# A state-space scan whose input product is contracted over 40 rows, with two banks for its sums

## The chip, the cores and the metric

One core of a Trainium2 chip runs the whole program. It has five engines: TensorE (PE in the profile, PEld for its weight loads), VectorE (DVE), ScalarE (ACT), GpSimd (POOL) and SyncE (SP), which here only issues DMAs. Each engine works through its own instructions in order and waits on semaphores for the others. The metric is the device time of one execution in microseconds. Matmuls read SBUF and write PSUM, which has eight banks of 128 x 512 float32.

## What is computed

Two sequences (B = 2) of L = 2048 steps with 256 channels go through a feed-forward block, a selective state-space block and a second feed-forward block. The middle block is the costly one. Cut to its core:

```python
dt = soft_clamp(softplus(xc @ W_dt.T + b_dt), 0.001, 0.1, 0.5)        # (2, 2048, 512)
Bp, Cp = xc @ W_B.T, xc @ W_C.T                                       # (2, 2048, 16)
dA = exp(soft_clamp(dt[..., None] * A, -8.0, 8.0, 0.5))               # (2, 2048, 512, 16)
def step(h, inp):                                                     # h: (2, 512, 16)
    h = h * dA_t + dB_t * x_t[:, :, None]                             # dB * x = (dt * x) * B
    nrm = sqrt(sum(h * h, axis=(1, 2), keepdims=True))
    fac = minimum(20.0 / (nrm + 1e-08), 1.0)
    h = where(t % 10 == 0, h * fac, h)
    y = einsum('bdn,bn->bd', h, C_t) + D_param * x_t
    return (h, y)
x_out = ys * (gate * sigmoid(gate)) @ W_out.T
```

The state is renormalised every tenth step, so the scan is cut into blocks of ten steps, and no block can start before the norm of the one before it is known.

## The kernel before

The kernel has three stages that hand over to each other. The **first stage** (`pre_stage`) takes 256 steps of both sequences at a time (8 tiles, `TILES`): feed-forward block, projections, convolution, dt, u = dt * x, and B and C in one product of 32 rows (`project_bc`), all stored to scratch DRAM. Its PSUM ring of four banks is filled in the order of the list `order`. The **scan stage** (`scan_stage`) does the recurrence. The **last stage** (`post_stage`) gates, projects, and runs the second feed-forward block.

The scan works in 410 **units** (`UNITS`): unit m is block j = m // 2 of ten steps of sequence b = m % 2. The state of a unit is 128 partitions x 64 rows x 11 places, one of the 11 being the carry from the block before. What each engine does in its turn m, in this order:

- PE: `total(m + 2)`, the sum of squares over partitions; `inputs(m + 2)`, the product u * B of the unit, four matmuls of 176 columns each out of the tile `ub`; if a piece is due, `turn_piece`; then one eighth of a `readout`.
- ACT: `squares(m + 2)`, usually two of the 64 tanh rows of the next chunk (`tanhs`), `decays(m + 4)`, and the copies out of PSUM (`copy_y`, `high_piece`) if due.
- DVE: `carry(m)` (L1135), the first half of the scan (L1145), `clamp(m + 1)` (L1129), the second half; then `low_piece` if due.
- POOL: `norm(m + 1)` (L938), then `weigh(m, 0)` and `weigh(m, 1)` (L948), which multiply the two halves of the new state by C into `hc`; then `mask_piece` if due.

A **readout** sums `hc` over the 16 state columns for a group of four blocks, eight units (`QB * B`), with 16 matmuls against the identity into the PSUM bank `psY`, two of them per unit. It runs one group behind. Its first matmul waits until ACT has copied the sum of the group before it out of the same bank (`y_copied`), and ACT does this copy at the end of the same turn, m % 8 == 0. `hc` has two buffers, so the first `weigh` of a group waits until the readout of two groups before is complete (`y_summed`).

The tile `ub` holds, for each of the ten steps, four rows (`SPLITS`): u and B are each split into a high and a low part, and all four products are summed by the contraction. So 40 of 128 partitions carry data; the other 88 were set to zero once. A row is 512 values of u and 176 of B, B standing at the place of its own step of eleven and zero elsewhere. These rows lie in DRAM (`scratch_ub`) and are made from **pieces** of 128 steps of one sequence: SP loads a piece of u and of B (`load_piece`), PE turns it (`turn_piece`, L835 for u and L836 for B), ACT copies the rounded high part (`high_piece`, L843, 528 columns), DVE subtracts it for the low part (`low_piece`, L847), POOL spreads B by a mask (`mask_piece`, L855), and SP stores all (`store_piece`). There are 32 pieces. Two are made in the first stage, thirty in the scan, one each twelve units (`piece_unit`): in turn m PE and ACT do their part, in turn m + 1 DVE and POOL.

At its block j = 4 SP also stores dt and u of the last tile, 1 MB each (`store_dt_u`). In the last ten units DVE and PE begin work of the last stage (`post.skip`, `post.gate`, `post.project`).

## Time and profile before

| | us |
|---|---|
| median of 3 runs | 1650.04 (1645.67, 1650.04, 1650.18) |
| profiled execution, its own time | 1644.98 |
| its span in the trace | 1643.1 |
| first stage, until the first scan instruction | 430 |
| scan, 410 units | 430 to 1428 |
| rest of the last stage | 1428 to 1643 |

| engine | busy, share of the span | busy in 900 to 1100 us |
|---|---|---|
| PE | 1461.6 (89%) | 173.4 of 200 |
| DVE | 1278.2 (78%) | 170.6 of 200 |
| ACT | 1112.3 (68%) | 165.8 of 200 |
| POOL | 986.4 (60%) | 176.6 of 200 |

The halves of the DVE scan (L1145) take 882 ns each on average, a half of the weighing on POOL (L948) 821 ns, the power for the norm (L938) 551 ns. Granted TensorE clock in the scan is mostly 0.97 to 1.00 of full speed. In the middle of the scan four engines are busy for 83 to 88% of the time, so shares alone don't say which one sets the pace; the order of events does.

### The profile page before, as it was taken

To read this page: it belongs to the slowest core of one execution; us is meant where nothing else is said; L and a number is where in the kernel's file an instruction comes from. 1 tells how busy PE (TensorE), PEld (TensorE's weight loads), DVE (VectorE), ACT (ScalarE), POOL (GpSimd) and SP (SyncE) were. 2 spreads that over 40 slices of the span, in tenths; PEclk is the share of its full clock that TensorE was granted. 3 is DMA by queue.
4 is the path that set the end of the run, shared out by engine and by line. 5 is a ranking of instruction groups with operands and counts; after the bars stand their busy time and mean duration, and the time that the engine had idled before them with its cause. 6 is when DMAs were issued, how large, how long until landed. Compare 5 with 4: busy or idle time off the path is not lost. (4 is left out here: it accounts for less than half of the span.)

```text
span 1643.1 us, 24197 instructions
## 1 busy us (share of the span) xinstructions
PE 1461.6 (89%) x6460; PEld 986.7 (60%) x6460; DVE 1278.2 (78%) x2555; ACT 1112.3 (68%) x2515; POOL 986.4 (60%) x1350
## 2 busy tenths in 40 slices
PE   6999999999688888888888888888888888999998
PEld 5555555554456566656665656665665665677776
DVE  7657656655578888888887888887888889877885
ACT  4355445557978888888887888887888874243333
POOL 1202222012479898989988889898998999700000
PEclk9999999999789999999999999999999999999999
DMA  7222355125565555656655565555655436465430
GB/s 251 77 79 91 117 146 143 66 92 189 164 182 158 162 152 140 172 149 168 160 154 151 137 174 133 158 161 141 178 153 155 135 98 198 122 208 171 137 116 26
DMA packets 232654, 236.84 MB, mean 144 GB/s; under 512 B 46120, under 2 KB 198376, under 8 KB 232520
## 3 DMA queue, kind: packets, MB, share of 16 engines
q1 hardware_dynamic: 231576, 233.99, 49.7%
q8 instruction: 54, 0.88, 0.2%
q10 hardware_dynamic: 944, 1.31, 0.2%
q14 instruction: 80, 0.66, 0.1%
HBM read 136.84 MB, written 98.68 MB: 143 GB/s over the span
## 5 line engine op out<-in xcount | busy, mean ns | idle before, releaser
L1145 DVE TENSOR_TENSOR_SCAN h<-decay,banks 128x352 f32<-128x352 f32 x820 | 710.5, 882 | 56.8 <-POOL hc L948 1.5
L948 POOL TENSOR_TENSOR hc<-h,bc 128x320 f32<-128x320 f32 x820 | 655.1, 821 | 30.6 <-PE banks L995 28.4
L995 PE MATMUL banks<-hc,w_ident 128*128 128x320 f32 (+1 forms) x1664 | 543.6, 452 | 47.6 <-ACT yc L1084 38.6
L1050 ACT ACTIVATE tb<-dtc,a 128x320 f32<-128x320 f32 (+1 forms) x832 | 416.3, 554 | 4.8 <-DVE x L562 4.8
L995 PEld LDWEIGHTS banks<-hc,w_ident 128*128 128x128 f32 x1664 | 291.8, 196 | 125.5 <-POOL hc L948 39.8
L1072 ACT ACTIVATE decay<-tb 128x640 f32<-128x640 f32 x410 | 296.3, 723 | 0.4
L938 POOL TENSOR_TENSOR rc<-qs,w_mhalf 128x1 f32<-128x1 f32 x410 | 225.9, 551 | 114.9 <-DVE qs L1129 106.0
L983 PE MATMUL banks<-ub 128*128 128x176 f32 x1640 | 283.9, 297 | 10.9 <-DMA ub<-scratch_ub 10.9
L976 PEld LDWEIGHTS banks<-sc_ss,sc_ones 128*128 128x128 f32 x820 | 134.6, 197 | 263.8 <-ACT sc_sq L1061 246.2
L1061 ACT ACTIVATE sc_sq<-h 128x64 f32<-128x64 f32 x410 | 128.1, 313 | 189.1 <-issue 100.0
L983 PEld LDWEIGHTS banks<-ub 128*128 128x128 f32 x1640 | 227.4, 201 | 12.2 <-DMA ub<-scratch_ub 11.2
L976 PE MATMUL banks<-sc_ss,sc_ones 128*128 128x1 f32 x820 | 151.4, 254 | 90.4 <-ACT sc_sq L1061 56.4
L244 POOL TENSOR_TENSOR ln_rz<-ln_vz,w_mhalf 128x4 f32<-128x4 f32 x8 | 13.9, 1736 | 281.0 <-DVE ln_vz L568 281.0
L1135 DVE TENSOR_SCALAR banks<-h,rc 128x64 f32<-128x64 f32 x410 | 136.6, 333 | 34.2 <-POOL rc L938 22.2
L330 PE MATMUL banks<-zT,win 128*128 128x512 f32 x256 | 115.3, 604 | 5.5 <-ACT gf L397 4.5
L338 PE MATMUL banks<-xc,wdt 128*128 128x512 f32 x256 | 112.4, 592 | 3.1 <-ACT sg L434 3.1
L1284 POOL TENSOR_TENSOR q_ln_rs<-q_ln_ve,w_mhalf 128x4 f32<-128x4 f32 x8 | 10.9, 1364 | 172.2 <-DVE q_ln_ve L1555 172.2
L1385 ACT ACTIVATE q_gf<-banks,w_b,w_a 128x512 f32<-128x512 f32 x64 | 49.9, 780 | 69.6 <-PE banks L1318 67.9
L330 PEld LDWEIGHTS banks<-zT,win 128*128 128x128 f32 x256 | 48.1, 192 | 68.2 <-issue 60.3
L338 PEld LDWEIGHTS banks<-xc,wdt 128*128 128x128 f32 x256 | 48.0, 190 | 58.6 <-issue 54.1
L1129 DVE TENSOR_SCALAR qs<-banks 128x1 f32<-128x1 f32 x410 | 55.5, 135 | 30.3 <-PE banks L976 30.0
L1061 ACT ACTIVATION_READ_ACCUMULATOR sc_sq<-h 128x1 f32 x410 | 77.0, 188 | 0.0
(117 smaller groups left out, 1562.1 us busy)
## 6 DMA issues: line engine op xcount, KB each, us to landing
ub<-scratch_ub SPq DMA_DIRECT2D x410, 107.5 KB
bc<-scratch_blk SPq DMA_DIRECT2D x205, 160.0 KB, 3.6
scratch_ub<-turned SPq DMA_DIRECT2D x64, 512.0 KB, 4.1
scratch_ub<-spread SPq DMA_DIRECT2D x64, 176.0 KB, 4.3
scratch_xc<-xc SPq DMA_DIRECT2D x8, 1024.0 KB, 4.8
scratch_sg<-sg SPq DMA_DIRECT2D x8, 1024.0 KB, 5.9
scratch_dt<-dt SPq DMA_DIRECT2D x8, 1024.0 KB, 5.9
scratch_u<-u SPq DMA_DIRECT2D x8, 1024.0 KB, 6.7
```

Of the source, the lines that this page charges most:

```text
L330: mm = pe.matmul(out, win[:, k, (m0 + m) * P:(m0 + m + 1) * P], zT[:, k, :], start=(k == 0), stop=(k == KD - 1))
L338: mm = pe.matmul(out, wdt[:, k, m * P:(m + 1) * P], xc[:, i % 2, k, :], start=(k == 0), stop=(k == KE - 1))
L938: pool.tensor_tensor(rc[:, b:b + 1], qs[:, b:b + 1], w.mhalf[:, 0:1], ALU.pow).then_inc(norm_ready, 1)
L948: pool.tensor_tensor(hc[:, pl % 2, x * kh * B * N:(x + 1) * kh * B * N, j % QB * S:(j % QB + 1) * S] .rearrange("p (c b n) e -> p c b n e" ...
L976: pe.matmul(psQ[:, b:b + 1], ones[:], ss[:, b:b + 1], start=True, stop=True).then_inc(sum_ready, 1)
L983: mm = pe.matmul(psI[m % B][:, c * N * W:(c + 1) * N * W], ub[m % URING][:, c * P:(c + 1) * P], ub[m % URING][:, E:], start=True, stop=True)
L995: mm = pe.matmul(psY[:, 0:KE * B * wide], w.ident[:], rhs, start=(n == 0), stop=(n == N - 1))
L1050: act.activation(tanh_rows(c, r), dtc[:, c % 2, k * B:(k + 1) * B, 0:blocks_of(c) * S].rearrange("p b (k e) -> p k b e", e=S), ACT.Tanh, s ...
L1061: act.activation(sq[:, b, :], state(m - B)[:, :, S], ACT.Square, accum_out=ss[:, b:b + 1]).then_inc(sq_ready, 1)
L1072: act.activation(decay[:, m % DRING].rearrange("p (g i e) -> p g i e", g=DB, e=W)[:, :, :, 1:], tanh_block(j, b), ACT.Exp, scale=DTA_HALF ...
L1135: dve.tensor_scalar(inp(m)[:, :, 0], state(m - B)[:, :, S], rc[:, b:b + 1], None, ALU.mult).then_inc(carry_ready, 1)
L1145: dve.tensor_tensor_scan(state(m).rearrange("p r e -> p (r e)")[:, half], decay[:, m % DRING, half], psI[m % B][:, half], 0.0, ALU.mult, A ...
```

## The change

- **40 rows.** `ub` has 40 partitions instead of 128, so `inputs` contracts over 40. The four memsets of 128 x 688 go.
- **Two sum banks.** `readout` p writes bank 2 or bank 5 in turns (`y_bank`) and waits for the copy of p - 2 (`y_before`). Bank 2 comes from the pieces, which now have bank 3 alone. `copy_y` moves from turns m % 8 == 0 to m % 8 == 2. At the end of the scan, after `LAST_EVEN`, only bank 5 is used.
- **Late weighing.** POOL weighs unit m - 1 in turn m, in one instruction of four by 16 by 10 instead of two of half the size. The parts of a readout move one turn later with it.
- **B from the first stage.** A new ring entry `("bt", i, 0)` in which PE turns B of a tile (four transposes of 16 rows, `turn_b`), ACT copies it (`copy_bt`), and POOL splits and spreads it (`spread_b`: a copy, a subtraction, four masks for each tile), around `norm2`. SP stores it (`store_b`). For the last tile the four masks are in POOL's turns 8, 12, 16 and 20 of the scan. A piece is now u alone, 512 columns, with no mask.
- **Pieces.** One each ten units. In its turn m and the three after it PE does one transpose each, after the readout; ACT copies 256 columns each in turns m + 4 and m + 5; DVE subtracts in turn m + 6.
- **SP.** dt and u of the last tile go out in eight stores of 256 KB at j = 1 to 8 (`store_last`).

```diff
@@ the first stage
+        if i >= 1:
+            order.append(("bt", i - 1, 0))
...
+            if i >= 2:
+                scan.store_b(sp, i - 2, 2, G)
+            if i >= 1:
+                scan.store_b(sp, i - 1, 0, 2)
             sp.wait_ge(xc_ready, 2 * (i + 1))
...
+            if i >= 1:
+                scan.spread_b(pool, i - 1, 0, 2)
             if i + 1 < TILES:
                 norm2(i + 1)
-            if i in (6, 7):
-                scan.mask_piece(pool, i - 6)
+            if i >= 1:
+                scan.spread_b(pool, i - 1, 2, G)
...
+        def turn_b(i):
+            out = fill(("bt", i, 0))
+            pe.wait_ge(ring_read, use["bc", i, 0] + 1)
+            for q in range(G):
+                mm = pe.transpose(out[:, q * N:(q + 1) * N], bcs[0:N, q * P:(q + 1) * P], w.ident[0:N, 0:N])
+            mm.then_inc(ring_done, 1)
@@ the scan
-    return 12 * (k - B) + 2
+    return 10 * (k - B)
...
+    return 2 if p % B == 0 and p <= LAST_EVEN else 5
...
+    return p - 2 if p <= LAST_EVEN + 1 else p - 1
...
-    ub = [own.put(f"ub{q}", [P, ROW], F32R) for q in range(URING)]
+    ub = [own.put(f"ub{q}", [SPLITS * S, ROW], F32R) for q in range(URING)]
...
+        for q in range(q0, q1):
+            if G * i + q >= 2:
+                pool.wait_ge(b_out[q % 2], 2 * 16 * ((G * i + q) // 2))
+            pool.tensor_tensor(
+                spread[:, q % 2], bts[:, :, q].bitcast(F32).unsqueeze(3).broadcast_to([P, 2, N, W]),
+                mask[:, (i * TT // P + q % 2) % (S // 2)].unsqueeze(1).unsqueeze(1).broadcast_to([P, 2, N, W]),
+                ALU.mult).then_inc(spread_done, 1)
...
-            if j == 4:
-                pre.store_dt_u(sp, TILES - 1)
+            if 1 <= j <= 2 * KE:
+                pre.store_last(sp, j - 1)
+            if j in (6, 8, 10, 12):
+                store_b(sp, TILES - 1, j // 2 - 3, j // 2 - 2)
...
-            weigh(m, 0)
-            weigh(m, 1)
-            if m - 1 in pieces:
-                mask_piece(pool, pieces[m - 1])
+            if m >= 1:
+                weigh(m - 1)
+            if m in (8, 12, 16, 20):
+                spread_b(pool, TILES - 1, m // 4 - 2, m // 4 - 1)
...
-                if p >= 1:
-                    pe.wait_ge(y_copied, p)
+                if y_before(p) >= 0:
+                    pe.wait_ge(y_copied, y_before(p) + 1)
...
-            p, part = m // (QB * B) - 1, m % (QB * B)
+            p, part = (m - 1) // (QB * B) - 1, (m - 1) % (QB * B)
             if p >= 0:
                 readout(p, part * each, (part + 1) * each)
...
+            for c in range(KE):
+                if m - c in pieces:
+                    turn_piece(pe, pieces[m - c], psT, c, c + 1)
...
-            if m % (QB * B) == 0 and m >= 2 * QB * B:
+            if m % (QB * B) == 2 and m >= 2 * QB * B:
                 copy_y(m // (QB * B) - 2)
-            if m in pieces:
-                high_piece(act, pieces[m], psT)
+            for x in range(2):
+                if m - KE - x in pieces:
+                    high_piece(act, pieces[m - KE - x], psT, x * E // 2, (x + 1) * E // 2)
...
-            if m - 1 in pieces:
-                low_piece(dve, pieces[m - 1], psT)
+            if m - KE - 2 in pieces:
+                low_piece(dve, pieces[m - KE - 2], psT)
```

On PE, in the scan, a piece stood in one turn. Before (L976 is `total`, L983 `inputs`, L835 and L836 the piece, L995 the readout):

```order
L976 MATMUL banks<-sc_ss,sc_ones 128x1
L983 MATMUL banks<-ub_100 128x176 x4
L835 MATMUL banks<-w_ident,piece 128x128 x4
L836 MATMUL banks<-w_ident,piece_b 128x32
L995 MATMUL banks<-hc,w_ident 128x320 x2
L976 MATMUL banks<-sc_ss,sc_ones 128x1
L983 MATMUL banks<-ub_101 128x176 x4
```

And now (L1060 is `total`, L1067 `inputs`, L1079 the readout, L897 one transpose of the piece):

```order
L1067 MATMUL banks<-ub_100 128x176 x4
L1079 MATMUL banks<-hc,w_ident 128x320 x2
L897 MATMUL banks<-w_ident,piece 128x128
L1060 MATMUL banks<-sc_ss,sc_ones 128x1
L1067 MATMUL banks<-ub_101 128x176 x4
L1079 MATMUL banks<-hc,w_ident 128x320 x2
L897 MATMUL banks<-w_ident,piece 128x128
L1060 MATMUL banks<-sc_ss,sc_ones 128x1
L1067 MATMUL banks<-ub_102 128x176 x4
```

The transposes stand one to a turn, behind the readout and not ahead of it; the order of total, inputs and readout is the same.

On POOL, in the scan, before (L938 is `norm`, L948 a half of `weigh`, L855 the mask of a piece):

```order
L938 TENSOR_TENSOR rc<-qs,w_mhalf 128x1
L948 TENSOR_TENSOR hc<-h,bc_97 128x2x16x10 x2
L938 TENSOR_TENSOR rc<-qs,w_mhalf 128x1
L948 TENSOR_TENSOR hc<-h,bc_97 128x2x16x10 x2
L855 TENSOR_TENSOR spread<-turned,mask 128x352
L938 TENSOR_TENSOR rc<-qs,w_mhalf 128x1
```

And now (L1021 is `norm`, L1032 `weigh`):

```order
L1032 TENSOR_TENSOR hc<-h,bc_99 128x4x16x10
L1021 TENSOR_TENSOR rc<-qs,w_mhalf 128x1
L1032 TENSOR_TENSOR hc<-h,bc_96 128x4x16x10
L1021 TENSOR_TENSOR rc<-qs,w_mhalf 128x1
L1032 TENSOR_TENSOR hc<-h,bc_96 128x4x16x10
```

One instruction stands between two norms where two stood, and the mask of the piece is gone from the row.

On ACT, in the scan, before (L843 is the copy of a piece, L1061 `squares`, L1050 the tanh rows, L1072 `decays`):

```order
L1072 ACTIVATE decay<-tb 128x64x10
L843 ACTIVATE turned<-banks 128x528
L1061 ACTIVATE sc_sq,sc_ss<-h 128x64
L1050 ACTIVATE tb<-dtc,a_110 128x16x2x10 x2
L1072 ACTIVATE decay<-tb 128x64x10
```

And now (L906, L1147, L1136, L1158 in the same sense):

```order
L1158 ACTIVATE decay<-tb 128x64x10
L906 ACTIVATE turned<-banks 128x256
L1147 ACTIVATE sc_sq,sc_ss<-h 128x64
L1136 ACTIVATE tb<-dtc,a_111 128x32x10 x2
L1158 ACTIVATE decay<-tb 128x64x10
L906 ACTIVATE turned<-banks 128x256
```

The copy of a piece is in two halves, a turn apart.

## Rows read from the trace of the kernel before

**Rows 1.** Timeline, one undisturbed unit: start, us, engine, line, what [idle before <-releaser].
```profile
955.99 0.34 DVE L1135 TENSOR_SCALAR banks<-h,rc 128x64 f32<-128x64 f32 x1
956.14 0.32 ACT L1061 ACTIVATE sc_sq<-h 128x64 f32<-128x64 f32 x1 [0.17 <-issue]
...
956.60 0.30 PEld L976 LDWEIGHTS banks<-sc_ss,sc_ones 128*128 128x128 f32 x2 [0.63 <-ACT sc_sq L1061]
...
957.26 0.13 DVE L1129 TENSOR_SCALAR qs<-banks 128x1 f32<-128x1 f32 x1
...
957.35 1.27 PE L995 MATMUL banks<-hc,w_ident 128*128 128x320 f32 x4
...
957.54 0.55 POOL L938 TENSOR_TENSOR rc<-qs,w_mhalf 128x1 f32<-128x1 f32 x1
...
958.12 0.34 DVE L1135 TENSOR_SCALAR banks<-h,rc 128x64 f32<-128x64 f32 x1
...
958.73 0.30 PEld L976 LDWEIGHTS banks<-sc_ss,sc_ones 128*128 128x128 f32 x2 [0.62 <-ACT sc_sq L1061]
```

**Rows 2.** Timeline, the start of a group of eight units.
```profile
982.56 0.33 DVE L1135 TENSOR_SCALAR banks<-h,rc 128x64 f32<-128x64 f32 x1
...
983.23 1.58 POOL L948 TENSOR_TENSOR hc<-h,bc 128x320 f32<-128x320 f32 x2 [0.70 <-PE banks L995]
...
985.13 1.31 PE L995 MATMUL banks<-hc,w_ident 128*128 128x320 f32 x4 [1.06 <-ACT yc L1084]
...
985.36 0.34 DVE L1135 TENSOR_SCALAR banks<-h,rc 128x64 f32<-128x64 f32 x1 [0.60 <-POOL rc L938]
```

**Rows 3.** Timeline, a unit in which a piece of u is turned.
```profile
997.37 0.60 PE L835 MATMUL banks<-w_ident,piece 128*128 128x128 f32 x4
...
997.90 0.13 PEld L836 LDWEIGHTS banks<-w_ident,piece_b 32*128 32x128 f32 x1 [0.17 <-issue]
...
998.08 1.34 PE L995 MATMUL banks<-hc,w_ident 128*128 128x320 f32 x4
...
998.18 0.61 ACT L843 ACTIVATE turned<-banks 128x528 fp32r<-128x528 f32 x1
...
998.83 0.71 DVE L847 TENSOR_TENSOR turned<-banks,turned 128x528 fp32r<-128x528 f32 x1 [0.61 <-ACT turned L843]
```

**Rows 4.** Timeline, a group of eight that begins just after a piece.
```profile
1003.71 0.34 DVE L1135 TENSOR_SCALAR banks<-h,rc 128x64 f32<-128x64 f32 x1
...
1004.15 2.28 PE L995 MATMUL banks<-hc,w_ident 128*128 128x320 f32 x4 [1.05 <-ACT yc L1084]
...
1007.75 0.34 DVE L1135 TENSOR_SCALAR banks<-h,rc 128x64 f32<-128x64 f32 x1
```

**Rows 5.** Busy us of PE, PEld, DVE, ACT, POOL (xcount), PEclk, DMA share, GB/s.
```profile
594.00:596.00 2.00, 1.69 (x4) 1.19 (x5) 1.09 (x2) 2.00 (x6) 1.39 (x2) 0.69 0.61 129
...
1294.00:1296.00 2.00, 2.00 (x8) 1.45 (x7) 0.86 (x3) 1.50 (x3) 0.88 (x2) 0.62 0.10 36
```

**Rows 6.** Instructions of L1135, 442 to 1427 us: ns min/median/max, first and last start.
```profile
L1135 DVE TENSOR_SCALAR banks<-h,rc x406: 322/333/342, 442.1 to 1426.4; 128x64 f32<-128x64 f32 x136
```

**Rows 7.** Who waited for whom, 442 to 1427 us: us in total, times, longest.
```profile
PE banks L995 <- ACT yc L1084: 38.0, 36, 1.1
...
DVE turned L847 <- ACT turned L843: 21.9, 30, 1.8
```

**Rows 8.** Groups by line and shape: busy us, mean ns | idle before.
```profile
L855 POOL TENSOR_TENSOR spread<-turned,mask 128x352 fp32r<-128x352 f32 x32 | 25.9, 809 | 8.2 <-DVE turned L847 8.2
...
L1084 ACT ACTIVATE yc<-banks 128x320 f32<-128x320 f32 x51 | 21.2, 416 | 15.3 <-PE banks L995 15.3
...
L253 POOL TENSOR_TENSOR ln_s<-ln_mv,ln_rs 128x4 f32<-128x4 f32 x8 | 1.7, 212 | 0.0
```

**Rows 9.** Timeline, early in the scan: PE waits for the rows of a unit.
```profile
464.40 0.69 PE L983 MATMUL banks<-ub 128*128 128x176 f32 x4 [4.39 <-DMA ub<-scratch_ub]
```

**Rows 10.** Timeline, first stage: PE before the gate projection.
```profile
253.56 7.13 PE L330 MATMUL banks<-zT,win 128*128 128x512 f32 x16 [0.60 <-ACT gf L397]
```

More of the change, by code:

```diff
@@ L142, in store_dt_u, with store_last, stored @@
         store(sp, "u", u[:], u_out, i)
+    def store_last(sp, k):
+        name, tile, ready, done = ("dt", dt, dt_ready, dt_out) if k < KE else ("u", u, u_ready, u_out)
+        c = k % KE
+        sp.wait_ge(ready, LAST + 1)
+        sp.dma_start(dram[name][:, c * B:(c + 1) * B, steps(LAST)],
+                     tile[:, c, :].rearrange("p (b t) -> p b t", b=B)).then_inc(done, 16)
+    def stored(i):
+        return 16 * (i + 1) if i < LAST else 16 * (LAST + KE)
     def dt_u(dve, i):
@@ L218, in sync @@
                 scan.load_units(sp)
+                scan.store_b(sp, LAST - 1, 2, G)
             if i == 3:
@@ L364, in tensor @@
             project(i, "x", 0)
+            if i >= 1:
+                turn_b(i - 1)
             if 1 <= i < LAST:
@@ L377, in tensor @@
             if i in (5, 6):
-                scan.turn_piece(pe, i - 5, psD.rearrange("p k c -> p (k c)"))
+                scan.turn_piece(pe, i - 5, psD[:, 0], 0, KE)
         project_bc(LAST)
+        turn_b(LAST)
     def scalar(act, scan, post):
@@ L485, in scalar @@
                 copy_x(i, 0, KE)
+                if i >= 1:
+                    copy_bt(i - 1)
             else:
@@ L493, in scalar @@
                 copy_x(i, 3, KE)
+                copy_bt(i - 1)
                 scan.tanhs(act, 0, 20, 33)
@@ L523, in scalar @@
         copy_bc(LAST)
-        scan.tanhs(act, 0, 52, KE * N)
+        scan.tanhs(act, 0, 52, 54)
+        copy_bt(LAST)
+        scan.tanhs(act, 0, 54, KE * N)
     def vector(dve, scan, post):
@@ L646, in vector @@
                 apply2(i + 1)
+            if i == 0:
+                scan.masks(dve)
             if i == 4:
                 scan.decay_scale(dve)
-                scan.masks(dve)
                 post.residual_steps(dve)
-    return Pre(sync, gpsimd, tensor, scalar, vector, dt_u, store_dt_u, order, use,
+    return Pre(sync, gpsimd, tensor, scalar, vector, dt_u, store_last, stored, order, use,
                ring_done, ring_read, sg_out, xc_out, r_out, u_out, dt_out, bc_out, u_ready, r_ready, x1_ready, t2_done,
@@ L673 @@
 ROW = E + N * W
+LAST_EVEN = (UNITS - 6) // (QB * B) - 2
+assert LAST_EVEN % 2 == 0
 Scan = namedtuple("Scan", """sync gpsimd tensor scalar vector load_first load_units tanhs decay_rates decay_scale masks
-    decay_ready y_out y_copied squares load_piece turn_piece high_piece low_piece mask_piece store_piece ut_lo""")
+    decay_ready y_out y_copied squares load_piece turn_piece high_piece low_piece store_piece ut_lo
+    spread_b store_b copy_bt b_split""")
 def chunk_of(j):
@@ L827, in load_piece @@
         sp.dma_start(piece[:], dram["u"].rearrange("p (c b) t -> p c b t", b=B)[:, :, b, t:t + P]).then_inc(piece_in, 16)
-        sp.dma_start(piece_b[:], dram["bc"][:, b, t:t + P]).then_inc(piece_in, 16)
-    def turn_piece(pe, k, out):
-        pe.wait_ge(piece_in, 32 * (k + 1))
-        if k >= 1:
-            pe.wait_ge(ut_lo, k)
-        for c in range(KE):
-            pe.transpose(out[:, c * P:(c + 1) * P], piece[:, c, :], w.ident[:])
-        pe.transpose(out[:, E:E + 2 * N], piece_b[:], w.ident[0:2 * N, 0:2 * N]).then_inc(ut_done, 1)
@@ L861, in store_piece @@
         t, b = k // B * P, k % B
[L862 removed]
         sp.wait_ge(ut_lo, k + 1)
         for r in range(2):
[L865 to L869 removed]
+            sp.dma_start(dram["ub"][b, t:t + P, 2 * r:2 * r + 2, 0:E], turned[:].bitcast(F32)).then_inc(ut_out, 16)
@@ L871, in masks, with store_b @@
+    def store_b(sp, i, q0, q1):
+        for q in range(q0, q1):
+            t = i * TT + q % 2 * P
+            sp.wait_ge(spread_done, G * i + q + 1)
+            for half in range(2):
+                sp.dma_start(
+                    dram["ub"][q // 2, t:t + P].rearrange("t (r h) x -> t r h x", h=2)[:, :, half, E:],
+                    spread[:, q % 2].bitcast(F32).rearrange("p r n e -> p r (n e)")).then_inc(b_out[q % 2], 16)
     def masks(dve):
-        for q in range(URING):
-            dve.memset(ub[q][:].bitcast(F32), 0.0).then_inc(ub_zero, 1)
@@ L908, in sync @@
                     load_unit(sp, m)
[L909 to L912 removed]
+            if j - 3 in after and after[j - 3] + 1 < PIECES:
+                load_piece(sp, after[j - 3] + 1)
             if j + RING - 1 < NB:
```

159 lines of the change are left out of this document (88 added, 71 removed).

## The prediction

> **What bounds the kernel now.** The scan fills about 1000 of 1643 us and holds nearly all of the change, so I read it first, in order of time, and not by busy shares, which are alike for four engines. [rows 1] is one undisturbed unit. DVE's carry begins at 955.99 and the next at 958.12, a period of 2.13 us, and DVE has no idle time in it. The others nearly fill the same period. ACT idles 0.17. PE's readout starts at 957.35, takes 1.27 and so ends at 958.62, and its next sum of squares starts at 958.73: a gap of 0.11, and since consecutive matmuls overlap by 0.07 (the four transposes of [rows 3] end at 997.97, the next matmul starts at 997.90), PE has about 0.18 to spare. The clamp starts 0.66 after the sum of squares, which takes about 0.4 of it, so a late sum costs DVE nothing up to about 0.25. POOL's norm starts at 957.54, 0.28 after the clamp, and ends at 958.09, just before the carry: POOL has next to nothing to spare.
>
> So DVE sets a floor of 2.13 us a unit. The 406 carries of [rows 6] span 984.3 us, or 2.43 for each of 405 periods. At 2.13 they would take 862.7. The remaining 121.6 us is what the change can touch. Read by the gaps between carries, it comes in few sizes:
>
> - Pieces, thirty. DVE waits 0.61 for ACT's copy, then works 0.71 [rows 3]; 1.30 on the carries. The wait was there 30 times [rows 7]. 30 x 1.30 = 39.
> - Starts of a group of eight, 51 of them by the count of L1084 [rows 8]. POOL's first weighing waits 0.70 for the readout to leave `hc`, so the norm and then the carry come late: from 982.56 to 985.36 is 2.80, 0.67 over the floor [rows 2]. 51 x 0.67 = 34.
> - In the same place PE waits 1.06 for ACT's copy of the old sum [rows 2], 36 times in the scan [rows 7]. In [rows 2] this costs nothing beyond the 0.67: DVE is late by POOL's delay anyway. It costs where a piece has just gone by [rows 4]: PE has idled before, the wait comes on top, and the four readout matmuls take 2.28 instead of 1.27. The carries are 4.04 apart, 1.91 over the floor, with some 0.1 behind it. The granted clock shows why: 0.69 and 0.62 of full speed, parts of the stretch at the lower level of 1.2 GHz [rows 5]; these two are the first and the last of 12 such places. Each costs about 1.3 more than an ordinary start: 12 x 1.3 = 16.
> - The last ten units, in which DVE already works for the last stage: 10. A start-up with late DMAs: 6; PE waited 4.39 for its rows [rows 9]. The rest, about 16, is late loads and units with four tanh rows.
>
> **The change part by part**, against the profiled execution's own 1645.0 us (span 1643.1 and 1.9 around it).
>
> *Late weighing in one instruction.* The two halves take 1.58 [rows 2]. A product of four columns on POOL takes 0.212 [rows 8], so most of 0.2 per instruction is fixed; taking 0.19, one instruction of both halves takes 1.45, 0.13 less. In an undisturbed unit this is worth nothing, as DVE is the floor. At a group's start it is worth 0.13, if POOL's wait stays. It stays: weighing and readout both move a turn later, so the weighing of unit 8n still stands one turn behind the readout that must clear `hc`.
>
> *40 rows.* The data and columns are the same, so I take no time off. What could be added is the passage between products of 40 and of 128 rows, twice a unit. The nearest row is the turning of B, 32 rows, among products of 128 [rows 3]: its weights are loaded after a gap of 0.17; its matmul starts at 997.90, 0.20 after the fourth transpose (997.37 and three steps of 0.11), and the readout's 0.18 after that, where transposes follow each other at 0.11. Both passages cost 0.20 + 0.18 - 0.22 = 0.16. Bounds are nothing and twice the 0.17 gap, 0.34. I take 0.16, measured on the same kind of passage. It fits into PE's 0.18, so the floor stays at 2.13, but the readout ends 0.16 later. At a group's start this gives -0.13 + 0.16 = +0.03, over 51 starts **+1.5**.
>
> Against this: the Trainium skill, "TensorE: Matmul & The Clock Gate", section "LDWEIGHTS (loading the stationary operand)", gives the load's time by columns and not by the rows contracted. The trace agrees for the load itself (0.13 with 32 rows), not for the gap ahead of it. By the rule alone the sum would have nothing for the passage; that is the first rival below.
>
> *Pieces.* DVE's wait of 0.61 goes: it subtracts a turn after the second copy. Its own 0.71 remains (0.69 for 512 of 528 columns). ACT's halves: 0.416 for 320 columns [rows 8] and 0.61 for 528 [rows 3] give 0.36 for 256. Less ACT's 0.17 a turn, ACT is late by 0.19, then 0.38, of which 0.25 is covered: 0.13 on DVE. PE's four transposes, 0.11 each on a queue with 0.02 left, come to 0.36 late, 0.11 beyond that cover, partly at once with ACT's. I take 0.9 a piece: 30 x (0.9 - 1.3) = **-12**. Ends: -18 (only the wait goes) and 0.
>
> *Two sum banks.* PE's wait of 1.06 goes in all 51 starts, but only the 12 places with the low clock are on the path. There PE would idle 0.7 for the piece and 0.7 for POOL, not twice about 1.05. I take ten of the twelve as gone: **-13**. Ends: -16 and 0.
>
> *Masks and B.* The 30 masks leave POOL in the scan, where they hid behind DVE's wait. The last tile's four return, 0.81 each [rows 8], with two small ones ahead. POOL has 0.04 + 0.13 to spare a unit: 4 x 0.64 + 0.5 = **+3**. In the first stage PE gets a `turn_b` per tile: four transposes of 16 rows, 0.20 + 3 x 0.11 + 0.18 = 0.7. In six tiles PE waits 0.60 before the gate projection for a gelu [rows 10], whose time DVE sets; that wait shrinks by as much. 6 x 0.1 + 2 x 0.7 = **+2**. On POOL two masks, 1.6, come ahead of the next `rstd1`; DVE then gets its rows just before it would wait for ACT's copy of x anyway. SP's waits in `store_b` stand ahead of `store_xc`, which is ready long after. If these covers fail, 1.6 a tile, 10 in all.
>
> *SP.* dt and u of the last tile in eight stores instead of 2 MB at once: the late rows of [rows 9] should mostly be in time. **-4** (0 to -6).
>
> *Ends.* `copy_bt` adds 0.3 to ACT ahead of the first unit. The readout lags one turn more: 1.2 when the scan ends. In the last six units, which PE bounds, 6 x 0.16 = 1. **+2.5**.
>
> Sum: 1.5 - 12 - 13 + 3 + 2 - 4 + 2.5 = -20, so 1625. The profiled execution lies at the low end of the runs shown (1645.7 to 1650.2), and the time to come may lie at either; half the difference, 2, gives **1627**.
>
> **The rivals.**
>
> *Free passages.* If 40 rows cost nothing, each start gains 0.13 (-6.6 instead of +1.5), a piece costs 0.83 (-14), and the two ends save 2: 1615. For it: the rule cited above. Against it: the gap in [rows 3]. With all covers holding and all twelve places gone, 1604.
>
> *The slow places stay.* The 12 places with the low clock remain because piece, group start and the passages still fall together: 1625 + 13 + 2 = 1640. For it: pieces now come every ten units and meet a group's start in many phases.
>
> *PE becomes the bound (slower).* If each passage costs a whole gap of 0.17, PE needs 2.13 - 0.18 + 0.34 = 2.29 a unit. 405 x 0.16 = 65 over the floor, and 120 transposes x 0.11 = 13. DVE then has 0.16 + 0.25 in hand at each of 81 pieces and starts, which gives back 33. Net +45 - 20 = +25: 1672. The kernel is slower than before once the passages cost more than about 0.26 a unit. Against it: the trace's matmuls moved by 0.16 in all, though with 32 columns and not 176 in flight.
>
> *The clock falls for lack of rows.* If a product of 40 rows keeps the array less occupied in the eyes of what grants the clock, every group start can become like [rows 4]: 39 more at 1.3 and none of the twelve gone, 1627 + 13 + 51 = 1691, and far more if it stays low. For it: the drops show that the scan is not far from it. The Trainium skill, same page, Part 1, says the clock follows "how busy the PE has been recently"; by that, rows don't matter and this doesn't happen. No row here shows a long stretch of products of few rows.
>
> *The change does not do what it says.* That PE's wait for the copy is off the path in most groups is already in the sum.
>
> **How the numbers follow.** Forecast (1610 to 1636) 0.44; free passages 0.26; slow places stay 0.11; PE the bound 0.12; clock 0.07. Below 1604 lies under 0.05. To leave out no more than 2 in 10, the range reaches up to most of the case with PE as the bound: 1604 to 1662. A change of 0.3%, about what a measurement of this kernel can tell from none, is 5 us: same is 1645 to 1655. Faster: the first three less a little, 0.76. Same, from the slow places and a half-costly passage, 0.09. Slower 0.15.
>
> **What would show it.** Carries 2.13 apart in undisturbed units: the floor holds; 2.2 or more throughout, with DVE idle for PE: PE is the bound. In `inputs`, a gap before the weight load of the first matmul and of the readout behind it: the passage. At a group's start: no PE wait for ACT, POOL still waiting 0.7 to 0.9 for PE, a carry 0.7 late. At a piece: no DVE wait for ACT, about 0.9. Weighing: one instruction of about 1.45. Few stretches below full clock after 480 us. First stage longer by about 2. I am wrong if DVE gains or loses work, if the granted clock falls often, or if POOL's new work in the first stage delays DVE.

## The result, and the profile after

| | us |
|---|---|
| before, median of 4 runs | 1648.47 (1645.67 to 1650.18) |
| after, median of 4 runs | 2191.14 (2189.95 to 2195.20) |
| ratio after / before, 95% interval | 1.330 (1.327 to 1.333) |
| profiled execution of after, its span | 2190.14, 2188.3 |
| predicted | 1627 (1604 to 1662) |

The kernel became 33% slower. From the page of after: busy time by engine; the granted clock of PE in 40 slices of the span, in tenths; shares of the chain that ended last, by engine; and three groups of instructions.

```profile
PE 2139.6 (98%) x6460; PEld 1520.6 (69%) x6460; DVE 1341.0 (61%) x2551; ACT 1123.6 (51%) x2553; POOL 934.1 (43%) x956
...
PEclk9999999955555555555555555555555555559999
...
PE 77%; DVE 2%; ACT 0%; issue 0%; POOL 0%; DVEq 0%; POOLq 0%; ACTq 0%
...
L1032 POOL TENSOR_TENSOR hc<-h,bc 128x640 f32<-128x640 f32 x410 | 591.1, 1442 | 138.7 <-PE banks L1079 133.6
...
L1067 PE MATMUL banks<-ub 40*128 40x176 f32 x1640 | 470.1, 435 | 0.0
...
L1216 DVE TENSOR_SCALAR qs<-banks 128x1 f32<-128x1 f32 x410 | 64.4, 157 | 463.8 <-PE banks L1060 463.7
```

PE is busy 98% of a span that is 545 us longer. Its instructions are not more, but slower: the four matmuls of a product take 1.16 us (below), where they took 0.69 in [rows 9]. DVE now waits 463.7 us in all for the sum of squares of L1060. The stretches show when (us of PE, PEld, DVE, ACT, POOL, granted clock, DMA share, GB/s):

```profile
0.00:450.00 450.00, 414.94 (x1366) 235.76 (x1366) 280.35 (x578) 252.70 (x388) 125.81 (x134) 0.98 0.47 148
450.00:500.00 50.00, 45.88 (x133) 34.89 (x133) 32.41 (x62) 34.04 (x88) 31.32 (x35) 0.50 0.51 165
...
1000.00:1300.00 300.00, 300.00 (x818) 221.01 (x818) 174.81 (x323) 162.17 (x419) 154.07 (x157) 0.50 0.34 99
...
1960.00:2188.00 228.00, 218.80 (x998) 171.02 (x998) 166.08 (x336) 75.24 (x107) 20.74 (x17) 0.99 0.39 124
```

From 430 us, where the scan begins, to 1963, a few us before its last carry, PE is granted 0.50, its lower level of 1.2 GHz, and in the middle it is busy 300 of 300 us. The first and the last stage run at full clock, as in before. The timeline of one unit of after, to be laid beside [rows 1]:

```profile
1701.12 0.43 PE L1060 MATMUL banks<-sc_ss,sc_ones 128*128 128x1 f32 x2
1701.48 1.16 PE L1067 MATMUL banks<-ub 40*128 40x176 f32 x4
...
1702.57 2.50 PE L1079 MATMUL banks<-hc,w_ident 128*128 128x320 f32 x4
...
1704.86 0.42 PE L1060 MATMUL banks<-sc_ss,sc_ones 128*128 128x1 f32 x2
```

The starts are 0.36, 1.09 and 2.29 apart, 3.74 from one sum of squares to the next, where DVE's floor is 2.13. All carries of after (ns min/median/max, first and last start):

```profile
L1222 DVE TENSOR_SCALAR banks<-h,rc x410: 309/334/339, 433.5 to 1970.2; 128x64 f32<-128x64 f32 x137
```

Between the first and the last of its 410 carries after spends 1536.7 us. In before it is 998.1, from 428.3 to the 1426.4 of [rows 6].

### The profile page after: what moved, and what is told of

The parts are those of the page before. It is cut to its first block, busy times and chain, and to the rows that moved or that the text cites. A ratio compares the mean times of both kernels' runs of the same rounds, so it can differ in the third digit from the quotient of the medians.

```text
span 2188.3 us, 24473 instructions
## 1 busy us (share of the span) xinstructions
PE 2139.6 (98%) x6460; PEld 1520.6 (69%) x6460; DVE 1341.0 (61%) x2551; ACT 1123.6 (51%) x2553; POOL 934.1 (43%) x956
## 4 chain that ended last, share of the span: by engine, by line
PE 77%; DVE 2%; ACT 0%; issue 0%; POOL 0%; DVEq 0%; POOLq 0%; ACTq 0%
PE banks L1079 45%; PE banks L1067 20%; PE banks L1060 4%; PE banks L1384 3%; PE banks L1405 2%; PE banks L1415 2%; PE banks L897 1%; DVE q_ln_st L1637 0%; DVE q_g L1546 0%; DVE q_x L1518 0%; PE banks L1425 0%; PE banks L1394 0%; DVE q_g L1544 0%; DVE q_ln_mv L1640 0%; DVE h L1232 0%
## 5 line engine op out<-in xcount | busy, mean ns | idle before, releaser
L1079 PE MATMUL banks<-hc,w_ident 128*128 128x320 f32 (+1 forms) x1664 | 1006.8, 760 | 0.6 <-ACT yc L1170 0.6
L1232 DVE TENSOR_TENSOR_SCAN h<-decay,banks 128x352 f32<-128x352 f32 x820 | 722.4, 882 | 55.5 <-ACT decay L1158 1.4
L1032 POOL TENSOR_TENSOR hc<-h,bc 128x640 f32<-128x640 f32 x410 | 591.1, 1442 | 138.7 <-PE banks L1079 133.6
L1079 PEld LDWEIGHTS banks<-hc,w_ident 128*128 128x128 f32 x1664 | 477.2, 317 | 222.5 <-issue 219.0
L1021 POOL TENSOR_TENSOR rc<-qs,w_mhalf 128x1 f32<-128x1 f32 x410 | 226.4, 552 | 620.5 <-DVE qs L1216 620.5
L1147 ACT ACTIVATE sc_sq<-h 128x64 f32<-128x64 f32 x410 | 129.1, 315 | 702.5 <-issue 659.8
L1067 PE MATMUL banks<-ub 40*128 40x176 f32 x1640 | 470.1, 435 | 0.0
L1136 ACT ACTIVATE tb<-dtc,a 128x320 f32<-128x320 f32 (+1 forms) x832 | 415.2, 552 | 4.9 <-DVE x L605 4.8
L1067 PEld LDWEIGHTS banks<-ub 40*128 40x128 f32 x1640 | 377.1, 318 | 6.1
L1060 PEld LDWEIGHTS banks<-sc_ss,sc_ones 128*128 128x128 f32 x820 | 259.0, 335 | 159.2 <-issue 145.6
L1216 DVE TENSOR_SCALAR qs<-banks 128x1 f32<-128x1 f32 x410 | 64.4, 157 | 463.8 <-PE banks L1060 463.7
L1158 ACT ACTIVATE decay<-tb 128x640 f32<-128x640 f32 x410 | 295.7, 722 | 0.4
L1060 PE MATMUL banks<-sc_ss,sc_ones 128*128 128x1 f32 x820 | 175.7, 284 | 11.4 <-ACT sc_sq L1147 10.8
L1147 ACT ACTIVATION_READ_ACCUMULATOR sc_sq<-h 128x1 f32 x410 | 76.6, 187 | 0.0
```

Of the source, the lines that this page charges most:

```text
L1021: pool.tensor_tensor(rc[:, b:b + 1], qs[:, b:b + 1], w.mhalf[:, 0:1], ALU.pow).then_inc(norm_ready, 1)
L1032: pool.tensor_tensor(hc[:, pl % 2, :, j % QB * S:(j % QB + 1) * S] .rearrange("p (c b n) e -> p c b n e", c=KE, b=B)[:, :, b], state(m)[:, ...
L1060: pe.matmul(psQ[:, b:b + 1], ones[:], ss[:, b:b + 1], start=True, stop=True).then_inc(sum_ready, 1)
L1067: mm = pe.matmul(psI[m % B][:, c * N * W:(c + 1) * N * W], ub[m % URING][:, c * P:(c + 1) * P], ub[m % URING][:, E:], start=True, stop=True)
L1079: mm = pe.matmul(banks[:, y_bank(p), 0:KE * B * wide], w.ident[:], rhs, start=(n == 0), stop=(n == N - 1))
L1136: act.activation(tanh_rows(c, r), dtc[:, c % 2, k * B:(k + 1) * B, 0:blocks_of(c) * S].rearrange("p b (k e) -> p k b e", e=S), ACT.Tanh, s ...
```

## The experiments

Three theories stood at the start. *Rows*: the clock stays down because the product uses 40 of the array's 128 rows. *Passages*: each change between products of different row counts stalls PE, and it is these short stalls that hold the clock down. *Another part*: the new order, with piece transposes spread over four turns, keeps PE from getting ahead. Below, "after128" is the changed kernel with the product over 128 rows again, and diffs are against it unless said otherwise. A time without a range was measured once.

### Back to 128 rows

Diff against after (left out: the waits on `mask_zero` go up by `URING` to match, and SP waits for it before its first loads):

```diff
-    ub = [own.put(f"ub{q}", [SPLITS * S, ROW], F32R) for q in range(URING)]
+    ub = [own.put(f"ub{q}", [128, ROW], F32R) for q in range(URING)]
...
-        sp.dma_start(ub[m % URING][:].bitcast(F32),
+        sp.dma_start(ub[m % URING][0:SPLITS * S, :].bitcast(F32),
...
+        for q in range(URING):
+            dve.memset(ub[q][:].bitcast(F32), 0.0).then_inc(mask_zero, 1)
```

> The changed kernel with one thing undone: the product u*B is contracted over 128 rows again, 88 of them zeros set once; late weighing, two sum banks, B from the first stage and the spread pieces stay. The result is complete. Theory (the 40 rows hold the granted clock at the lower level, 0.50 in the changed kernel's scan): the clock returns to 0.97 or more and the time is near the 1627 us of the forecast, 1605 to 1640. Rival (something else in the change keeps the clock low, such as the order of the matmuls, the single transposes or the missing waits): the clock stays near 0.5 and the time stays above 2100 us.

Measured: **1604.34** (1603.75 to 1609.19), 0.974 of before (0.971 to 0.978). Everything but the 40 rows gains 2.6%; the 40 rows alone cost 587 us. Granted clock by slice and the group of its weighings:

```profile
PEclk9999999999969999999999999999999999899999
...
L1035 POOL TENSOR_TENSOR hc<-h,bc 128x640 f32<-128x640 f32 x410 | 594.0, 1449 | 32.3 <-PE banks L1082 32.0
```

and all its carries (ns min/median/max, first and last start):

```profile
L1225 DVE TENSOR_SCALAR banks<-h,rc x410: 309/333/346, 435.1 to 1385.0; 128x64 f32<-128x64 f32 x137
```

The first and last carry are now 949.9 apart, 586.8 less than in after: the whole difference lies in the scan.

Where the two part can be seen, since both enter the scan at 0.50: the clock falls at 430 in after and at 435 in after128. After, at the start of the scan, where PE is all but idle:

```profile
434.00:438.00 4.00, 0.58 (x3) 0.57 (x3) 2.69 (x4) 3.97 (x10) 0.18 (x1) 0.50 0.54 134
```

Windows of after128:

```profile
464.00:468.00 4.00, 4.00 (x13) 3.02 (x13) 3.17 (x7) 3.04 (x8) 3.25 (x5) 0.50 0.28 91
468.00:472.00 4.00, 4.00 (x23) 3.14 (x22) 3.42 (x8) 3.67 (x11) 2.93 (x4) 0.89 0.79 236
```

and of after in the same place:

```profile
464.00:468.00 4.00, 4.00 (x12) 2.90 (x11) 2.72 (x5) 3.31 (x9) 2.52 (x3) 0.50 0.48 155
468.00:472.00 4.00, 4.00 (x13) 2.94 (x12) 2.17 (x4) 2.75 (x8) 2.62 (x3) 0.50 0.33 102
```

In both, PE has stopped waiting by 464 and is busy in full. With 128 rows its clock rises in the next window, with 40 it stays down for the rest of the scan. The other kernels below part in the same way: all that use 96 or 128 rows here, and before too, rise for the first time between 458 and 476 us, the one with 64 rows at 521, and those with 40 rows, in all four matmuls of a product or in three, not for hundreds of us.

### Before, with 40 rows alone

Diff against before:

```diff
-                mm = pe.matmul(psI[m % B][:, c * N * W:(c + 1) * N * W], ub[m % URING][:, c * P:(c + 1) * P],
-                               ub[m % URING][:, E:], start=True, stop=True)
+                mm = pe.matmul(psI[m % B][:, c * N * W:(c + 1) * N * W], ub[m % URING][0:SPLITS * S, c * P:(c + 1) * P],
+                               ub[m % URING][0:SPLITS * S, E:], start=True, stop=True)
```

> The kernel before with one thing changed: the product u*B is contracted over the 40 rows that hold data; the tile stays 128 rows with its zeros, and nothing else moves. The result is complete. Theory (40 rows alone do it): the clock falls to 0.5 in the scan and the time is 2150 to 2250 us. Rival (it needs the other parts of the change as well): clock about 0.97 and 1640 to 1670 us.

Measured: **2162.79**, 514 over before, with the mean clock at 0.665. The new order is not the cause.

Its clock is low from 428 to 1937 us, but not without a break. It rises at 1083, 1203 and 1247 and stays up for 34, 3 and 31 us. The first of these:

```profile
1080.00:1084.00 4.00, 4.00 (x15) 2.76 (x14) 1.81 (x4) 2.44 (x6) 2.38 (x4) 0.58 0.10 28
1084.00:1090.00 6.00, 6.00 (x30) 4.15 (x29) 5.60 (x13) 4.57 (x14) 5.58 (x9) 1.00 0.47 123
```

So 40 rows make a rise rare here, not impossible. Each of the three follows within about 4 us the start of a piece's four transposes (1080.17, 1198.87, 1243.63), which have 128 rows; in after, where they stand one to a turn, there is no rise at all. Most of the thirty pieces bring none, and whether the transposes are the cause was not tried.

### 40 rows from the middle of the scan on

Here, and in the reverse of it below, `ub` has 128 partitions as in after128.

```diff
+        def rows(m):
+            return P if m < 200 else SPLITS * S
...
-                mm = pe.matmul(psI[m % B][:, c * N * W:(c + 1) * N * W], ub[m % URING][:, c * P:(c + 1) * P],
-                               ub[m % URING][:, E:], start=True, stop=True)
+                mm = pe.matmul(psI[m % B][:, c * N * W:(c + 1) * N * W], ub[m % URING][0:rows(m), c * P:(c + 1) * P],
+                               ub[m % URING][0:rows(m), E:], start=True, stop=True)
```

> The changed kernel, contracting over 128 rows with zeros up to unit 199 and over 40 rows from unit 200 on. The result is complete. If a steady scan at 40 rows cannot hold the upper level of the clock, it falls within some us of unit 200 and stays low: about 1627 + 210 x 1.3 = 1900 us. If 40 rows only keep a clock that is low from rising again, the fall comes at the first later disturbance (a piece with a group's start, or a late load), some 50 us or more after unit 200. If neither holds, about 1627 us.

Measured: **1861.50**. The first product of 40 rows starts at 898.96. The windows after that:

```profile
920.00:968.00 48.00, 44.59 (x216) 32.09 (x215) 43.04 (x87) 42.41 (x112) 40.51 (x43) 1.00 0.55 160
968.00:972.00 4.00, 4.00 (x14) 2.97 (x14) 3.04 (x7) 3.56 (x9) 2.81 (x3) 0.62 0.88 283
...
1000.00:1600.00 600.00, 600.00 (x1620) 444.30 (x1619) 353.39 (x647) 304.23 (x790) 312.16 (x319) 0.50 0.29 81
```

PE alone, a wait after which the clock stays up, and the one after which it falls:

```profile
938.34 0.38 PE L1063 MATMUL banks<-sc_ss,sc_ones 128*128 128x1 f32 x2 [0.92 <-ACT sc_sq L1153]
...
965.97 0.38 PE L1063 MATMUL banks<-sc_ss,sc_ones 128*128 128x1 f32 x2 [0.84 <-ACT sc_sq L1153]
...
969.04 2.50 PE L1085 MATMUL banks<-hc,w_ident 128*128 128x320 f32 x4
```

A high clock is kept for 70 us with 40 rows, PE busy 44.6 of 48 us, and undisturbed units are 2.13 apart. It falls after PE has waited 0.84, and does not come back in 600 us of unbroken work. The length of that wait alone doesn't explain the fall: a wait of 0.92 had passed without one 28 us before. With 128 rows waits of this size do less: between 480 and 1340 us after128's PE waits 0.8 to 1.6 more than thirty times, and its clock falls once (at 882, after 1.63) and is back in 3.4 us.

### 40 rows first, 128 from the middle on

The same edit the other way round (`SPLITS * S if m < 200 else P`).

> The changed kernel, contracting over 40 rows up to unit 199 and over 128 rows with zeros from unit 200 on: the reverse of the run that changed to 40 rows at unit 200. The result is complete. Theory (40 rows can keep an upper clock but not raise a low one; 128 rows raise it): the clock is low from the start of the scan to about unit 200, then rises within some us and stays up: 1604 + 200 x 1.35 = 1870 to 1900 us. Rival (once low for long it stays low whatever follows): about 2190 us.

Measured: **1888.45**. The first product of 128 rows starts at 1181.87:

```profile
1178.00:1182.00 4.00, 4.00 (x14) 3.04 (x12) 2.17 (x4) 1.95 (x5) 1.95 (x2) 0.50 0.45 157
1182.00:1186.00 4.00, 4.00 (x19) 3.16 (x18) 3.40 (x7) 2.24 (x7) 2.98 (x4) 0.79 0.22 59
1186.00:1190.00 4.00, 3.99 (x23) 2.95 (x22) 3.73 (x7) 3.65 (x11) 3.14 (x4) 1.00 0.46 95
```

PE is as busy before as behind. Only the rows change, and the clock rises within 2 us. With the run before, this shows that it is the rows, whichever units they are in.

### 64 and 96 rows

`ub` has 64 or 96 partitions instead of 128, the rest zeros as in after128.

> The changed kernel with the product contracted over 64 rows, 24 of them zeros. The result is complete. If what counts is the groups of 32 rows that are touched, 40 rows already touch two groups, so 64 rows give the same as 40: clock 0.5, about 2190 us. If it is the number of rows, 64 stands between 40 and 128 and may do better: part of the scan at the upper level, 1640 to 2100 us.

> The changed kernel with the product contracted over 96 rows, 56 of them zeros. The result is complete. With 40, 64 and 128 rows the time was 2191, 2070 and 1604 us. Theory (the number of rows in the array counts, gradually): 96 rows hold the upper level nearly always, 1604 to 1640 us. Rival (anything short of all 128 rows lets the clock fall in large parts of the scan): 1750 us or more.

Measured: **2069.97** with 64 rows (mean clock 0.703) and **1605.59** with 96 (0.978), which is after128's time. Clock by slice, 64 rows first:

```profile
PEclk9999999965656555555555957965555555569999
```

```profile
PEclk9999999999969999999999999999999998899999
```

With 64 rows the clock rises here and there, stays up for 14 to 96 us, and falls again. With 96 it behaves as with 128.

### One matmul of four with 128 rows

Diff against after, with `ub` of 128 partitions as in after128; `inputs` takes `rows(c)` partitions for its matmul c:

```diff
+        def rows(c):
+            return P if c == 0 else SPLITS * S
```

> The changed kernel; of the four matmuls of each product one is contracted over 128 rows (88 zeros), three over 40. The mean is 62 rows. The result is complete. Theory (rows are summed over the work done): as with 64 rows in all four, about 2070 us with some stretches at the upper level. Rival (one product of 128 rows right behind the sum is enough to keep the array counted as full): clock 0.97 and about 1610 us. Other rival (each matmul of few rows is what counts): 2150 us or more, no stretch at the upper level.

Measured: **2248.01**, mean clock 0.646, and no stretch in which the clock rises. The passages of row counts are two a unit, as in after, but the first now stands inside the product: from the sum to the readout PE takes 1.58 where after takes 1.43, and 409 times this 0.15 is 60, about the 57 us that the run is over after. Whether rows are added up over matmuls, with 248 here a little short of the 256 of the 64-row run, or are looked at in another way, these two runs don't tell.

### Passages without few rows

A matmul of 40 rows and 2 columns ahead of each product, overwritten by it:

```diff
+                if c == 0:
+                    pe.matmul(psI[m % B][:, 0:2], ub[m % URING][0:SPLITS * S, 0:P],
+                              ub[m % URING][0:SPLITS * S, E:E + 2], start=True, stop=True)
```

> The changed kernel with 128 rows, and ahead of each product one more matmul of 40 rows and 2 columns, whose result is overwritten by the product. It makes PE pass from 128 rows to 40 and back once a unit, as the contraction over 40 rows does, with all real products at 128 rows. Theory (the rows of the products keep the clock up or not, the passages cost 0.17 us of PE time a unit): clock 0.95 or more, 1604 to 1680 us, passages plus 0.1 for the extra matmul on an engine with 0.18 to spare. Rival (the gaps at the passages are what lets the clock fall): clock near 0.5, above 2100 us.

Measured: **1635.43**, 31 over after128, with the mean clock at 0.969 against 0.981. The clock is nowhere near 0.50 as a whole, so passages alone don't hold it down, and the theory of passages falls. They do not leave it alone either. Here PE is busy in full at 0.50, in a stretch that after128 runs at full clock:

```profile
896.00:920.00 24.00, 24.00 (x72) 18.66 (x72) 12.83 (x25) 11.93 (x31) 10.23 (x11) 0.50 0.26 61
```

In all the clock is low for 55 us after 480, against 20 in after128. So in this one run, with every product at 128 rows, the passages or the small matmul itself seem to make a fall last longer; which of the two wasn't tried. They add 0.28 a unit here (medians of undisturbed units), no less than the real ones do, which makes this a fair test of them. The price of the real ones at full clock, first from after128, PE alone:

```profile
641.09 0.38 PE L1063 MATMUL banks<-sc_ss,sc_ones 128*128 128x1 f32 x2
...
641.34 0.66 PE L1070 MATMUL banks<-ub 128*128 128x176 f32 x4
...
641.84 1.27 PE L1082 MATMUL banks<-hc,w_ident 128*128 128x320 f32 x4
```

and from the kernel with 40 rows from the middle on, while its clock was still at 1.00:

```profile
942.94 0.38 PE L1063 MATMUL banks<-sc_ss,sc_ones 128*128 128x1 f32 x2 [0.34 <-ACT sc_sq L1153]
...
943.25 0.68 PE L1073 MATMUL banks<-ub 40*128 40x176 f32 x4
...
943.87 1.34 PE L1085 MATMUL banks<-hc,w_ident 128*128 128x320 f32 x4
```

The steps are 0.25 and 0.50 with 128 rows, 0.31 and 0.62 (mostly 0.61) with 40, and the four readout matmuls take 1.34 instead of 1.27. Each unit so has three losses, 0.06, 0.11 and 0.07: 0.25 from the sum to the start of the last readout matmul (1.83 instead of 1.58, medians of undisturbed units). With 96 rows all of this is as with 128.

### One sum bank

```diff
-    return 2 if p % B == 0 and p <= LAST_EVEN else 5
+    return 5
...
-    return p - 2 if p <= LAST_EVEN + 1 else p - 1
+    return p - 1
...
-            if m % (QB * B) == 2 and m >= 2 * QB * B:
+            if m % (QB * B) == 1 and m >= 2 * QB * B:
```

> The changed kernel with 128 rows (1604 us), and with one sum bank again: every readout in bank 5, its first matmul waits for the copy of the sum before, which ACT makes at the end of turn m % 8 == 1. The result is complete. The forecast's term for the second bank was 13 us (10 of 12 places with a fallen clock): 1612 to 1622 us, with PE waits of about 1 us for ACT's copy in some 50 places and a clock that falls in about ten. Rival (the wait is off the path since DVE or POOL is late anyway): 1602 to 1608 us.

Measured: **1635.08** (1628.38 to 1638.38), 31 more than after128 in medians, 24 to 34 between the ends of its range and that median. Its waits, 442 to 1427 us (us in all, times, longest):

```profile
PE banks L1082 <- ACT yc L1173: 45.5, 43, 1.1
...
DVE qs L1219 <- PE banks L1063: 27.9, 37, 1.8
```

In after128 the first wait is gone and the second is 9.6 in all, 19 times; in before DVE waited 27.9 for the sum too, 34 times. After 480 us the clock is below full at 13 places with one bank, and at three with two.

### Weighing in two halves

The product into `hc` by two instructions of 320 columns instead of one of 640.

> The changed kernel with 128 rows (1604 us), with the weighing in two instructions of half the size again; it still stands a turn late. The result is complete. The forecast had one instruction 0.13 us shorter than two, worth 0.13 only at group starts: 51 x 0.13 = 7 us more at most, 1606 to 1613 us. Rival (POOL sets the pace, as it has almost nothing to spare): 410 x 0.13 = 50 us more, about 1655 us.

Measured: **1611.04** (1609.93 to 1613.31), 6.7 more in medians; the nearest runs of the two kernels are 0.7 apart and the farthest 9.6. One instruction takes 1.449 (L1035 above), the two took 1.58 [rows 2].

### A piece in one turn

All four transposes of a piece in one turn, and ACT's copy and DVE's subtraction as in before; first with the transposes behind the readout, as this diff of PE's part has it, then ahead of it:

```diff
-            for c in range(KE):
-                if m - c in pieces:
-                    turn_piece(pe, pieces[m - c], psT, c, c + 1)
+            if m in pieces:
+                turn_piece(pe, pieces[m], psT, 0, KE)
```

> The changed kernel with 128 rows (1604 us), with a piece in one turn again: four transposes on PE and one copy of 512 columns on ACT in turn m, the subtraction on DVE in turn m + 1, still every ten units. The result is complete. The forecast had 0.4 us a piece for the spreading: 30 x 0.4 = 12 us more, 1613 to 1622 us, and a DVE wait of about 0.6 us for ACT at each piece. Rival (what a piece gained came with the mask that left POOL): 1602 to 1608 us.

> As the run with a piece in one turn (1654 us, 2.2 us a piece), but with the four transposes ahead of the turn's readout, where the kernel before had them, and not behind it. The result is complete. Theory (the loss there came from the transposes standing behind the readout, 1.2 us, which ACT's copy and then DVE waited for): a piece costs 1.3 us as before the change, DVE waits about 0.6 for ACT, 1613 to 1622 us; the difference to 1604 is what the spreading is worth. Rival (ACT is late for another reason, such as its copy of the sums a turn later): about 1654 us again.

Measured: **1654.31** (8 runs, 1650.30 to 1657.98) behind and **1618.40** (1618.03 to 1620.16) ahead. Who waited, 442 to 1427 us, behind first:

```profile
DVE turned L912 <- ACT turned L907: 55.9, 30, 5.1
...
ACT turned L907 <- PE banks L898: 38.2, 28, 4.6
```

```profile
DVE turned L912 <- ACT turned L907: 25.7, 29, 4.0
```

and of after128, from its first carry to its last:

```profile
DVE turned L912 <- ACT turned L907: 6.6, 28, 0.7
```

Spreading a piece over turns is worth 14 us against one turn with the transposes ahead of the readout, as in before. Behind the readout they cost 36 more: ACT waits for them, and DVE for ACT.

### The readout ahead of its last turn

The eight turns of a readout take 3, 2, 2, 2, 2, 2, 2 and 1 of its matmuls, so that `hc` comes free earlier relative to POOL's first weighing (the last group, behind the loop, starts one matmul later to match):

```diff
-                readout(p, part * each, (part + 1) * each)
+                readout(p, part * each + (part > 0), (part + 1) * each + (part < QB * B - 1))
```

> The changed kernel with 128 rows (1604 us), with the sixteen matmuls of a readout spread over its eight turns as 3, 2, 2, 2, 2, 2, 2, 1 and not two in each. The result is complete. POOL's first weighing of a group waits for the last of them; it ends about 0.6 us sooner. If that wait is what still costs about 0.55 us at each of 51 group starts, 15 to 25 us are gained: 1580 to 1590 us. Rival (PE has no room for a third matmul, 0.6 us, in the first turn and DVE waits there instead): 1600 to 1610 us.

Measured: **1601.28** (1597.71 to 1601.80), 0.970 of before (0.968 to 0.973), the fastest of all. The waits, 442 to 1427 us:

```profile
POOL hc L1035 <- PE banks L1082: 9.8, 37, 2.0
...
DVE qs L1219 <- PE banks L1063: 15.4, 24, 1.5
```

POOL's wait falls from 29.7 in after128 (434 to 1386 us) to 9.8, as expected, but DVE's for PE rises from 9.6 to 15.4: a turn with three readout matmuls fills PE, and the clock is below full more often (44 us in all after 480 us, against 20). So of the 15 to 25 us expected only 3 came; the intervals of the two ratios overlap, though the runs don't (after128's fastest is 1603.75).

## Why the prediction was wrong, step by step

**The step that failed** is "40 rows. The data and columns are the same, so I take no time off", with the passage as the only possible cost. It priced the edit by what PE executes and not by what clock it executes at. The fourth rival had the mechanism, but its price of 1691 let the clock fall at 39 more group starts and come back each time. What happened is its last clause, "far more if it stays low": the clock is low when the scan begins, since it falls at 427 to 436 us in all of these kernels, where PE waits for up to 4 us at a time, and with 40 rows it does not rise. The sum then is not one of stalls. A unit takes PE about 3.74 instead of DVE's 2.13; 409 times 3.74 is 1530, and 1536.7 was measured. This price could have been worked out ahead, by doubling PE's 1.95 in [rows 1] (2.13 less the 0.18 to spare) to 3.9, and the 0.07 it stood at was far too low for a term with no row behind it.

In rows: the clock is 0.50 over 300 us with PE busy 300 of 300. The Trainium skill, "TensorE: Matmul & The Clock Gate", Part 1, says the clock follows "how busy the PE has been recently"; read as busy time, as the prediction read it, this is contradicted. Its section "Why this matters for your kernels" says a lone matmul of 32 rows takes the time of one of 128; that agrees at equal clock (0.68 for four of 40 rows, 0.66 of 128), and not here as a whole (1.16 for four of 40 rows at the lower level).

**The rest of the change** was read nearly right. after128 has no passages, so by the prediction's own terms it is the case of free passages, 1615; 1604 was measured. What the carries take over 2.13 us each, in us:

| | before | after128 |
|---|---|---|
| thirty pieces | 43.0 | 28.6 |
| starts of a group of eight (units m with m % 8 = 1 or 2) | 48.7 | 18.9 |
| first units | 9.2 | 5.8 |
| last 18 units | 10.3 | 14.7 |
| the rest | 15.7 | 10.7 |
| all | 126.9 | 78.7 |

Of these 48 us the first stage takes 7 back: the first carry comes at 428.3 in before and at 435.1 in after128. By the prediction's terms:

- *Passages*: mis-sized, 0.25 a unit and not 0.16. The two gaps are right (0.17), but the 0.07 by which the readout behind them is longer was left out, though [rows 3] has it, 1.34 against the 1.27 of [rows 1]. The Trainium skill's rule that a weight load takes its time by columns (the same page, "LDWEIGHTS (loading the stationary operand)") gives none of the 0.25. PE's slack was taken too small as well: from the start of the last readout matmul to that of the next sum it is 0.55 in after128's undisturbed units, and 0.27 where nothing is waited for, so 0.28 was to spare and not 0.18. The two errors cancel: with 40 rows at full clock a unit kept its 2.13, with 0.03 left. That the floor held is partly luck.
- *Pieces*: 0.88 in the median without passages, 0.83 forecast for that case; 14 us gained, 14 forecast there.
- *Late weighing*: 1.449 against 1.45, and 6.7 us for the two halves against 51 x 0.13 = 6.6. Where a group start costs anything it is mostly 0.53, by the forecast 0.67 - 0.13 = 0.54; but many cost nothing, and all of them together 18.9 us, where 51 x 0.54 is 28.
- *Two sum banks*: mis-sized. 24 to 34 against 13, with 16 as the end. All twelve places with a low clock did go, but one bank costs elsewhere too: DVE waits 27.9 us for the sum of squares, in before as with one bank, and 9.6 with two banks. The prediction had booked PE's wait of [rows 2] at nothing wherever POOL was late as well. The run with one bank has pieces every ten units, not every twelve, so its 31 us need not be what before lost by it.
- *Masks and B*: +2 for the first stage was too little, its end comes 7 late (5 in after). What of that are the transposes, the masks or the copy of B wasn't tried. The last tile's four masks, put at +3, make DVE wait for POOL's norm three times near the start of the scan, 0.98, 0.48 and 0.48: about 2.
- *Ends*: the last 18 units lose 4.4, forecast 2.5 with passages and less without. Why wasn't tried.
- *SP*: the first units gain 3.4, forecast 4.
- *PE as the bound*: it is, but by its clock and not by the passages. *Slow places stay*: none of the twelve did. The three low places of after128 are others: one behind a late load (PE waits 1.63), as in before, and two in the last 18 units. *The change does not do what it says*: each step stands where the diff puts it.

Taken out singly, the second bank, the one weighing and the spreading are worth 31, 7 and 14 us; with 3 for the first units, less 7 and 4, that comes to the 44 between before and after128. The forecast for free passages had 32. With 24 to 34 for the first of these alone, so close a sum is partly luck.

## What to carry to other kernels

Rows of the array that multiply zeros are not waste if they keep the clock up: before cutting a contraction where PE has little to spare, price it at both clock levels, and look at what clock the stretch begins with. The 88 rows cost no time (0.66 us for four matmuls with them, 0.68 without), so leaving them out had nothing to gain on PE and could only lose there. If few rows are wanted, try a step between first: 96 rows cost nothing here and 64 cost 464 us more than that.

## What was not expected of the hardware

- With the same columns in the same order the kernel takes 2191 us with 40 rows in the product, 2070 with 64, 1606 with 96 and 1604 with 128; the mean clock is 0.65, 0.70, 0.98 and 0.98.
- The clock has a memory: with 40 rows it stayed at 1.00 for 70 us and stayed at 0.50 for 600. The same work per unit gives either, by what went before. It isn't the same work per us: a unit takes 2.13 at the upper level and 3.74 at the lower, so PE does 1.8 times as much in a us while the clock is up, which may be what lets it stay there. That is argued, not shown.
- It isn't a lock: in before with 40 rows alone the clock rose three times.
- A passage from 128 to 40 or 64 rows and back costs 0.25 at full clock, 0.06 going in, 0.11 coming out and 0.07 in the matmuls behind it, and nothing with 96 rows.
- What is counted (rows summed over matmuls, or otherwise) is open: one matmul of four at 128 rows did not raise the clock once.
